# Neighbourhood attention and an FFT convolution on one core: output quarters at the end, and an earlier third row at the start

## The reference

```python
# layer 0: 7x7 neighbourhood attention, 4 heads, and an MLP
xn = layernorm(x, ln1_w, ln1_b)
q, k, v = split(xn @ w_qkv + b_qkv)
x = x + (softmax(q * scale @ windows(k) + rpb) @ windows(v)) @ w_proj + b_proj
x = x + gelu(layernorm(x, ln2_w, ln2_b) @ w_fc1 + b_fc1) @ w_fc2 + b_fc2
# layer 1, on tokens t = (4, 3136, 128)
t = t + (ln(t) @ Wq + bq) * sum_over_tokens((ln(t) @ Wk + bk) * (ln(t) @ Wv + bv))
u = ln(t)
# four spectral filters over the first 1/1, 1/2, 1/4, 1/8 of the tokens; hard choice of one
U = irfft(rfft(phi) * rfft(u)); s = sum_k U[k] * sigma[k]**0.25 @ M_phi[k] + sum_i shift(u, i) @ M_u[i]
t = t + sum(stack(s for each length) * weights)
```

## Time and profile before

| | |
|---|---|
| median of 3 runs | 1770.49 us (1768.07 to 1772.65) |
| the profiled execution's own time | 1771.29 us |
| its span in the profile | 1770.0 us |
| mean granted TensorE clock | 0.977 |
| TensorE busy | 1652.3 us, 93% |
| VectorE, ScalarE, GpSimd busy | 75%, 69%, 42% |

### The profile page before, as it was taken

One profiled execution on the slowest core, in us unless ns is written; L12 is line 12 of the kernel. 1 busy time (PEld: TensorE's weight loads), 2 busy tenths in 40 slices (PEclk: granted clock), 3 DMA queues, 4 the chain that ended last, 5 costly groups with the idle time before them and its releaser, 6 DMA issues.

```text
span 1770.0 us, 76295 instructions
## 1 busy us (share of the span) xinstructions
PE 1652.3 (93%) x32219; PEld 1346.7 (76%) x32219; DVE 1320.9 (75%) x3860; ACT 1219.7 (69%) x2712; POOL 743.7 (42%) x979
## 2 busy tenths in 40 slices
PE   5899999998999998897899999999999999999997
PEld 3577776666676766797788888888888888888674
DVE  2677788888876876687567777777777777776886
ACT  5788888887877755555767777777777677775232
POOL 6555555655554554121324443434453345531011
PEclk8899999999999998898999999999999999999998
DMA  4432333333332322377613333343233333335874
GB/s 119 118 85 77 98 94 83 89 103 98 90 100 77 98 73 54 103 224 249 204 37 85 72 79 67 65 90 84 65 76 74 71 85 76 75 69 148 199 148 73
DMA packets 278979, 175.90 MB, mean 99 GB/s; under 512 B 92082, under 2 KB 272480, under 8 KB 277042
## 3 DMA queue, kind: packets, MB, share of 16 engines
q1 hardware_dynamic: 263968, 151.00, 30.7%
q0 software_dynamic: 12288, 19.63, 7.8%
q10 hardware_dynamic: 2384, 0.40, 0.2%
HBM read 100.41 MB, written 83.46 MB: 104 GB/s over the span
## 4 chain that ended last, share of the span: by engine, by line
PE 67%; DVE 14%; issue 5%; POOL 5%; ACT 5%; DMA 2%; SPq 1%; DVEq 0%; POOLq 0%; ACTq 0%
PE banks L1410 21%; PE banks L1388 11%; PE banks L1391 10%; PE banks L413 6%; DVE zone L619 4%; PE banks L1709 3%; PE banks L1696 3%; PE banks L407 2%; DVE st L606 2%; PE banks L372 2%; DVE W L661 1%; ACT zone L563 1%; PE banks L420 1%; PE banks L362 1%; PE banks L460 1%
## 5 line engine op out<-in xcount | busy, mean ns | idle before, releaser
L1450 DVE COPY Gm<-banks 128x448 f32<-128x448 f32 x896 | 549.2, 637 | 183.0 <-PE banks L1388 108.8
L1429 ACT ACTIVATE Gm<-banks 128x448 f32<-128x448 f32 x896 | 515.9, 625 | 212.7 <-PE banks L1388 154.7
L1410 PE MATMUL banks<-Gm,U 128*32 128x128 f32 x12544 | 513.7, 274 | 8.4 <-POOL U L1505 6.9
L1410 PEld LDWEIGHTS banks<-Gm,U 128*32 128x32 f32 x12544 | 336.3, 110 | 50.6 <-issue 43.6
L1391 PE MATMUL banks<-V,zone 118*32 118x224 bf16 x7040 | 292.8, 259 | 3.3 <-issue 3.3
L881 POOL TENSOR_TENSOR W<-W,mx 128x280 f32<-128x280 f32 x196 | 130.2, 664 | 222.7 <-DVE mx L668 222.3
L1388 PE MATMUL banks<-V,zone 118*128 118x224 bf16 x1824 | 215.9, 261 | 1.3 <-ACT qT L1215 0.5
L1525 POOL DMA_DIRECT2D Yd<-Zd x102 | 78.8, 773 | 297.6 <-DMA Yd<-Zd 273.0
L1391 PEld LDWEIGHTS banks<-V,zone 118*32 118x32 bf16 x7040 | 192.6, 96 | 5.1 <-issue 4.1
L1388 PEld LDWEIGHTS banks<-V,zone 118*128 118x128 bf16 x1824 | 156.0, 98 | 49.6 <-issue 39.5
L527 ACT ACTIVATE W<-W,mx 128x140 f32<-128x140 f32 x392 | 156.2, 402 | 0.3
(11 more groups left out here) (193 smaller groups left out, 2654.0 us busy)
## 6 DMA issues: line engine op xcount, KB each, us to landing
W<-Vd SPq DMA_DIRECT2D x392, 49.0 KB
Yd<-YS SPq DMA_DIRECT2D x28, 448.0 KB, 4.8
Zd<-YS SPq DMA_DIRECT2D x56, 224.0 KB, 3.3
UL<-Ud SPq DMA_DIRECT2D x27, 448.0 KB, 4.5
Yd<-Zd POOLq DMA_DIRECT2D x95, 112.0 KB, 3.3
YL<-Yd SPq DMA_DIRECT2D x40, 196.0 KB
zone<-Mbf SPq DMA_DIRECT2D x28, 256.0 KB
Vd<-W SPq DMA_DIRECT2D x56, 112.0 KB
```

What stands on the lines that cost most here:

```text
L1410: ins = e.matmul(p[32 * x:32 * x + 32, :], self.U7[(2 * P + ch) % 3][:, sl, 8 * (3 - q):8 * (3 - q) + 32], self.Gm[:, par, r:r + 2, :], st ...
L1429: e.activation(dst, src, ACT.Copy).then_inc(S["gm_act"], 1)
L1450: v.tensor_copy(dst, src).then_inc(S["gm_dve"], 1)
```

## The change

Two parts. At the start, `q_mom`, `q_root` of the third row (g = 2) stand three units earlier in the list and its `q_norm` two units earlier; `q_pre` of the rows 0, 1, 2 stands at u = 5, 7 and 13 in place of 14, 15 and 16, and waits for the loads `d_bv` (which now include `b_proj`, moved four places ahead among ScalarE's loads) in place of all of `d_rest`. At the end, pairs 5 and 6 are accumulated in pieces (two DMAs with the two kept quarters, and one DMA for each turned quarter, both k together), and of pair 7 the quarters 0 and 3 (step 14) go through ScalarE, RN[1] and accumulating DMAs too; only quarters 1 and 2 (step 15) are left for VectorE, RX and SyncE, which writes them in three DMAs in place of six.

```diff
         q0 = LEAD + NJ * (g - 2) - 2 if g > 1 else 3 * g
-        put(q0, rests="q_mom", n=g)
-        put(q0 + 1, rests="q_mom q_root", n=g, half=1)
-        put(q0 + 2, rests="q_norm", n=g)
-        put(q0 + 3, rests="q_norm", n=g, half=1)
-        put(max(q0 + 4, LEAD + 3 + g if g < 3 else 0), rests="q_pre", n=g)
+        early = 3 if g == 2 else 0
+        put(q0 - early, rests="q_mom", n=g)
+        put(q0 + 1 - early, rests="q_mom q_root", n=g, half=1)
+        put(q0 + 2 - early + early // 3, rests="q_norm", n=g)
+        put(q0 + 3 - early + early // 3, rests="q_norm", n=g, half=1)
+        put(5 if g == 0 else q0 + 4, rests="q_pre", n=g)
...
         e.dma_start(self.rowb[:, 0, :], row_of(D["b_qkv"][256:384])).then_inc(S["d_bv"], 16)
+        e.dma_start(self.rowb[:, 1, :], row_of(D["b_proj"])).then_inc(S["d_bv"], 16)
...
             elif k == "q_pre":
                 if n == 0:
-                    q.wait_ge(S["d_rest"], self.n_rest)
+                    q.wait_ge(S["d_bv"], 32)
...
+def out_both(A, n, a):
+
+    b, pp = n // 2, n % 2
+    return A[b, :, 256 * pp:256 * pp + 256].rearrange("(k a p) x -> p k a x", p=G, a=4)[:, :, a]
...
-        for t in range(1, 19):
+        for t in range(1, 18):
             if 3 <= t and t + 1 < 16:
                 self.keep_half(e, t + 1)
-            if 3 <= t < 17:
+            if t >= 3:
                 self.turned(e, t - 3)
-            if t <= 14:
+            if t <= 15:
                 self.kept(e, t - 1)
...
-            if t == 15:
-                self.last_kept(v, 14)
-        self.last_turned(v, 14)
-        self.last_kept(v, 15)
-        self.last_turned(v, 15)
+        self.last_kept(v)
+        self.last_turned(v)
...
-        for n in range(7):
+        for n in range(5):
             q.wait_ge(S["kept"], 4 * n + 4)
             q.wait_ge(S["turned"], 4 * n + 4)
-            self.add_rows(q, n)
+            self.add_rows(q, n, slice(0, 4))
+        q.wait_ge(S["kept"], 24)
+        self.add_rows(q, 5, slice(0, 2))
+        q.wait_ge(S["turned"], 22)
+        self.add_row(q, 5, 3)
+        q.wait_ge(S["turned"], 24)
+        self.add_row(q, 5, 2)
+        q.wait_ge(S["kept"], 28)
+        self.add_rows(q, 6, slice(0, 2))
+        q.wait_ge(S["turned"], 26)
+        self.add_row(q, 6, 3)
+        q.wait_ge(S["kept"], 30)
+        self.add_row(q, 7, 0)
+        q.wait_ge(S["turned"], 28)
+        self.add_row(q, 6, 2)
+        q.wait_ge(S["turned"], 30)
+        self.add_row(q, 7, 3)
...
+    def add_row(self, q, n, a):
+
+        q.dma_start(out_both(self.out, n, a), self.RN[n % 3][:, :, a], accum_op=ALU.add).then_inc(self.S[f"d_o{n % 3}"], 16)
...
-        for count, rows in ((4, slice(0, 4, 3)), (6, slice(1, 2)), (8, slice(2, 3))):
+        e.wait_ge(S["last"], 2)
+        e.dma_start(out_both(self.out, 7, 1), self.RX[:, :, 0]).then_inc(S["d_last"], 16)
+        for count, k in ((3, 1), (4, 0)):
             e.wait_ge(S["last"], count)
-            for k in range(2):
-                e.dma_start(out_rows(self.out, 7, k)[:, rows], self.RX[:, k, rows]).then_inc(S["d_last"], 16)
+            e.dma_start(out_rows(self.out, 7, k)[:, 2:3], self.RX[:, k, 1:2]).then_inc(S["d_last"], 16)
```

More of the change, by code:

```diff
@@ L475, in load_columns @@
         e.dma_start(D["wsel"][:, 16:17], col_of(D["c_id"][128])).then_inc(S["d_rest"], 16)
-        for i, a in enumerate((D["b_proj"], D["b_fc2"], D["bq"], D["bk"], D["bv"])):
-            e.dma_start(self.rowb[:, 1 + i, :], row_of(a)).then_inc(S["d_rest"], 16)
+        for i, a in enumerate((D["b_fc2"], D["bq"], D["bk"], D["bv"])):
+            e.dma_start(self.rowb[:, 2 + i, :], row_of(a)).then_inc(S["d_rest"], 16)
     def scalar(self, e):
@@ L644, in vector @@
                 if n == 0:
-                    v.wait_ge(S["d_bv"], 16)
+                    v.wait_ge(S["d_bv"], 32)
                 if n >= 2:
@@ L1859, in whole, with last_kept, last_turned @@
         v.tensor_tensor(self.NT[t % 2][:, :, :], self.SC[:, :, 0, :], self.SC[:, :, 1, :], ALU.add).then_inc(S["tsum"], 1)
[L1861 to L1865, removed]
+    def last_kept(self, v):
+        w, rx = self.D["wsel"], self.RX
+        v.wait_ge(self.S["tsum"], 16)
+        v.wait_ge(self.S["d_last"], 32)
         for k in range(2):
-            at = 8 + 4 * k + q
-            v.scalar_tensor_tensor(rx[:, k, q], self.NT[q][:, k, :], w[0:G, at:at + 1], rx[:, k, q], ALU.mult, ALU.add
+            at = 8 + 4 * k + 1
+            v.scalar_tensor_tensor(rx[:, k, 0], self.NT[1][:, k, :], w[0:G, at:at + 1], rx[:, k, 0], ALU.mult, ALU.add
                                    ).then_inc(self.S["last"], 1)
-    def last_turned(self, v, t):
-        w, q, rx, p = self.D["wsel"], t % 2, self.RX, self.bank("turn", t)
-        v.wait_ge(self.S["tmm"], t + 1)
+    def last_turned(self, v):
+        w, rx, p = self.D["wsel"], self.RX, self.bank("turn", 15)
+        v.wait_ge(self.S["tmm"], 16)
         for x, k in ((0, 1), (1, 0)):
-            at = 8 + 4 * k + 3 - q
-            v.scalar_tensor_tensor(rx[:, k, 3 - q], p[:, 256 * x:256 * x + 256], w[0:G, at:at + 1], rx[:, k, 3 - q],
+            at = 8 + 4 * k + 2
+            v.scalar_tensor_tensor(rx[:, k, 1], p[:, 256 * x:256 * x + 256], w[0:G, at:at + 1], rx[:, k, 1],
                                    ALU.mult, ALU.add).then_inc(self.S["last"], 1)
@@ L1905, in gpsimd, with add_rows @@
         q.wait_ge(S["d_t2c"], 112)
-        for n in range(7):
+        for n in range(5):
             q.wait_ge(S["kept"], 4 * n + 4)
             q.wait_ge(S["turned"], 4 * n + 4)
-            self.add_rows(q, n)
-    def add_rows(self, q, n):
+            self.add_rows(q, n, slice(0, 4))
[15 more added lines that the diff above has]
+        self.add_row(q, 7, 3)
+    def add_rows(self, q, n, rows):
         for k in range(2):
-            q.dma_start(out_rows(self.out, n, k), self.RN[n % 3][:, k], accum_op=ALU.add).then_inc(self.S[f"d_o{n % 3}"], 16)
+            q.dma_start(out_rows(self.out, n, k)[:, rows], self.RN[n % 3][:, k, rows], accum_op=ALU.add
+                        ).then_inc(self.S[f"d_o{n % 3}"], 16)
+    def add_row(self, q, n, a):
+        q.dma_start(out_both(self.out, n, a), self.RN[n % 3][:, :, a], accum_op=ALU.add).then_inc(self.S[f"d_o{n % 3}"], 16)
     def sync(self, e):
@@ L1929, in sync @@
                 for k in range(2):
-                    e.dma_start(self.RX[:, k], out_rows(self.out, 7, k)).then_inc(S["d_last"], 16)
-        for count, rows in ((4, slice(0, 4, 3)), (6, slice(1, 2)), (8, slice(2, 3))):
+                    e.dma_start(self.RX[:, k], out_rows(self.out, 7, k)[:, 1:3]).then_inc(S["d_last"], 16)
+        e.wait_ge(S["last"], 2)
+        e.dma_start(out_both(self.out, 7, 1), self.RX[:, :, 0]).then_inc(S["d_last"], 16)
+        for count, k in ((3, 1), (4, 0)):
             e.wait_ge(S["last"], count)
-            for k in range(2):
-                e.dma_start(out_rows(self.out, 7, k)[:, rows], self.RX[:, k, rows]).then_inc(S["d_last"], 16)
[L1935 to L1938, removed]
+            e.dma_start(out_rows(self.out, 7, k)[:, 2:3], self.RX[:, k, 1:2]).then_inc(S["d_last"], 16)
+        e.wait_ge(S["d_o0"], 32 * 2 + 64)
+        e.wait_ge(S["d_o1"], 32 * 2 + 32)
+        e.wait_ge(S["d_last"], 32 + 48)
+        e.wait_ge(S["d_o2"], 32 + 64)
 INVERSE_SIGNALS = "idft half gh bf fixed rows tdif tsum tmm turned kept d_o0 d_o1 d_o2 d_last last".split()
```

4 lines of the change are left out of this document (2 added, 2 removed).

## The result

| | before | changed |
|---|---|---|
| median | 1771.09 us (1765.72 to 1772.81, 6 runs) | 1758.13 us (1751.48 to 1763.56, 6 runs) |
| ratio, 95% interval | | 0.9932 [0.9913, 0.9952] |
| profiled execution, its span | 1771.29, 1770.0 us | 1758.10, 1756.8 us |

The change takes 0.55 to 0.68% off, some 10 to 12 us, where 8.2 were forecast. Single executions of the changed kernel spread over 12 us, so an interval of the ratio is worth more here than any one execution.

A forecast was written before the change was run, and what follows sets the result against it. With TensorE busy 93% of the span, the prediction held that only the two ends could give something: 3.0 us at the start plus 5.2 at the end, 8.2 off, for 1762.5 us; range 1758.0 to 1767.0.

The forecast's parts named there:

- The detour by row 2: Start: ScalarE idles 3.73 us for row 2's root; with its moments earlier, the transposes come 3.17 us sooner.
- I keep the lower value: Start: the gain is put at 3.0 us, not the 4.3 us expected if TensorE's clock stays at 2.4 GHz.
- rival B: Start: the clock stays up, giving 4.3 + 5.2 = 9.5 us off, 1761.0 us; chance 0.12.
- GpSimd's three `q_pre` ... are worth nothing of themselves: Start: the three `q_pre` between the first `snorm`, 3 x 1.26 us, stood in idle time, so moving them gains nothing.
- nothing tied to the clock on the wall that I can find: Behind the start: every engine follows the same list; the first load of V for `out` has 5 us left.
- The end, 5.2 us: End: pairs 5 and 6 mostly leave earlier, less DMA work remains, and the span ends 5.2 us sooner.
- VectorE's 1.0 us: End: VectorE loses two `last_kept` and two `last_turned`, gaining about 1.0 us in all.
- Halving pair 7: End: SyncE writes two quarters of pair 7, not four: 1.6 us of full DMA share where it was 3.2.
- The price of an accumulated quarter: End: each accumulated quarter of a pair costs the DMA engines 1.46 us of full share.
- A: Rival: later waits absorb the start's 3 us and only the end counts, 1765.3 us; chance 0.16.
- C: Rival: the end is not shorter, quarters queue and SyncE's issues stall as before, 1766.5 us; chance 0.10.
- D: Rival: small accumulating DMAs in GpSimd's queue do not overlap, making it slower, about 1783 us; chance 0.03.

The follow-up runs named there:

- e5: Kernel before plus sixteen transposes of the identity on TensorE ahead of `q_turn` of row 2; 1773.13 us, ratio 1.0021 to the kernel before.
- e1: Kernel before with only the start part of the change; 1765.91 us, ratio 0.9978 to the kernel before.
- e10: The changed kernel unaltered, run and profiled once more; 1757.66 us, ratio 0.9945 to the kernel before.
- e3: Kernel before with row 2's moments and norm sooner and `b_proj`'s load ahead, but the three `q_pre` left where they were; 1775.95 us, one execution.
- e2: Kernel before with only the end part of the change; 1763.72 us, ratio 0.9963 to the kernel before.
- e6: Changed kernel, but pairs 5 and 6 accumulated whole as before, pair 7 still halved; 1762.98 us, one execution.
- e7: Changed kernel, pairs 5 and 6 still split, but pair 7 as before (all on VectorE, six plain DMAs); 1764.07 us, one execution.
- e9: Changed kernel with three quarters of pair 7 written plain and one accumulated; 1758.63 us, ratio 0.9947 to the kernel before.
- e4: Kernel before with only the three `q_pre` sooner and `b_proj`'s load ahead, row 2's moments not moved; 1769.96 us, one execution.

## Why the prediction came out as it did

The forecast of 1762.5 us had the sign and the order of the effect. It fell short by 4.4 us against 1758.13 and by 4.8 against 1757.66. Of these 1.7 to 2.8 came from the start (4.7 and 5.8 us in the two traces for 3.0); the rest is within the spread of the runs. The range went down to 1758.0: the first median lies 0.13 us inside it and the second 0.34 outside, so that the range held was luck.

**The detour by row 2: right.** The root was to be ready at 20.9, and was at 20.95; `q_norm` was to start at 21.49, and started at 21.13; the transposes at 23.75 came at 23.37, the scores at 24.85 at 24.58. These rows are 0.3 to 0.4 us better than forecast, most of which is a projection of row 1 that came 0.26 us sooner (18.81 for 19.07). That isn't of the change: the transposes ahead of it took 0.65 us for 0.91, and they are as short (0.60) in e5, whose list is that of before up to there. The cover for `q_pre` of row 1 was there too: the root's wait ahead of 19.01 was for VectorE's moments (0.45 us).

**"I keep the lower value" for the clock: wrong; rival B was the right one.** L342 was forecast at 26.03 and came at 25.22. Of these 0.81 us the scores ahead of it had 0.27 already, and most of the rest is that they took 0.71 and not 1.18 us; to `turn` of tile 0 the shift grew by another 1.3 us as L342 and L344 ran at full clock. B counted 0.87 us for the L341 pair alone, and so its bound (4.3) was too low as well: 5.0 at 35 us. The reason given for the lower value, the load of V, was no bound: e1's first `out` waited 0.51 us for it at 31.61, e10's not at all, and the next tile's scores were 4.9 and 5.0 us ahead. The Trainium skill's rule in TensorE: Matmul & The Clock Gate, section Why this matters for your kernels, says that idle gaps between bursts bring the clock down. In direction these rows agree: with the idle stretch ahead of 24 us cut from 1.68 to 0.87 us, the granted clock stayed up, and sixteen filling matmuls (e5) did the same. By that rule alone the prediction's sum for the start was 4.3 us.

**"GpSimd's three `q_pre` ... are worth nothing of themselves": wrong.** It was true of the kernel before, where `q_pre` waited for 1.05 us behind a chain that was as late. It is false of the change: `Wv`'s load lands at about 30 us by its own queue, and once the first `snorm` is 3.4 us ahead (24.50 for 27.94) and the load 1.1 us later, this wait grows to 5.55 us and takes nearly all of it back (e3). With row 2 early, freeing the `q_pre` was worth 4.9 us (6.1 in e1, 1.2 in e3). The same step failed in "nothing tied to the clock on the wall that I can find": `Wv` was such a thing, and it stood in the rows. The prediction's total wasn't hit by this only because the change removes that very wait. Had it been the moments alone, the same argument would have forecast 3.0 us where the trace keeps 1.2.

**The end, 5.2 us: right**, 5.25 and 5.45 in the traces of the changed kernel and 4.9 in e2, against before's tail, which is the shortest of five; against the longest 5.8 and 6.0. VectorE's 1.0 us was 1.22; the last VectorE instruction was to end 4.8 us before the span (1764.8 - 1760.0) and ended 4.74 before it. The reason given was right for pairs 5 and 6: moving them out of the way is everything (e6, e7). Halving pair 7 was part of the same sum and was thought to help; it is worth nothing that can be measured. So the sum's total was right with one term too many: that the halved pair was needed for it is not so. The price of an accumulated quarter, 1.46 us of full DMA share against 0.8 for a plain one, fits with e9, where one such quarter exchanged for a plain one took 0.6 to 0.8 us off, but isn't shown by it.

**Rivals.** A (the start is absorbed) fell: at 58 and at 513 us the shift of a kernel is the same within 0.25 us, and e1's interval excludes 1. At the inverse stage the same 3 us were to be seen; the shifts there, -1.8 to -10.1, can't tell. C (the quarters queue up) fell: three issues in 1.5 us and a tail 5.45 us shorter. D (small accumulating DMAs don't overlap) fell: from issue to landing a quarter took 4.7 us in the middle of seven, more than the 4.5 from which D was to decide, but two issued behind one another at 1748.95 and 1749.80 had both landed by 1756.1; they overlap. D's time also came from a misread row: the 6.5 us in the earlier trace rows are the median of pair 5's two DMAs (5.6 and 7.4 us), issued at 1747.10. Pair 6's, at the end itself, took 7.8 and 10.3. The Trainium skill's rule in DMA: Bandwidth & Descriptors, Rules for kernel authors, that small transfers should be joined, points the wrong way in this place: joining them (e6) costs 4.4 to 4.6 us of tail, since the joined DMA has to wait for its last quarter while the DMA engines stand idle (share 0.00 over 1734 to 1741 and 1747.5 to 1749.2).

## What to carry to other kernels

Where transfers end a program, look at when their data become ready, not only at how long they move: a transfer in pieces that starts under the last computation beats a whole one behind it, and once the DMA engines are free again the plain writes' issues shrink by themselves. When a chain of instructions is moved ahead, list every wait behind it that hangs on a load, with its landing time, even waits of 1 us: the shift turns into exactly such a wait. Undo each part of a change on the chip in both directions; here one part kept 1.2 us alone, the other nearly nothing of its own, and both together 6; a third, in the same patch, was worth nothing measurable. And take a second trace of the same program before explaining 1 us: a difference can be the granted clock's place in time, as in e4, or lie in the trace of the kernel before.

## What the runs showed of the hardware

- Issues on SyncE took longer while another queue's transfers ran: six DMAs took 7.91 us to issue while pair 6 was being accumulated (before), and 2.81 us (0.33 to 0.42 each) when it was not (e7).
- An accumulating DMA of 196 KB landed 4.7 us after its issue (median of seven in the changed kernel). The two of 392 KB of a pair took 5.6 and 7.4 us under TensorE's work (pair 5, before), and 7.8 and 10.3 at the end, where SyncE's writes ran with them (pair 6, before); in e6 the median was 8.7.
- The low-clock stretches of one program lie in different places from one execution to the next (0.99 and 0.54, then 0.89 and 0.85 over the same two windows), and this moves instructions by 1 us within the first 70 us.
